# A selective-scan layer on one core: two elementwise additions moved to DMAs, eight states instead of six added up by DMAs, and the order of the step written anew

## What is computed

```python
mod = (_silu(L0_c) @ L0_wmod).reshape(B, 6, 1, -1)          # sa, ca, ga, sb, cb, gb
h = _layernorm(x) * (1 + ca) + sa
xz = h @ w_in.T + b_in;  x_ssm, z = split(xz);  z = silu(z)
dt = softplus(x_ssm @ w_dt.T + b_dt)
Bm, Cm = x_ssm @ w_B.T + b_B, x_ssm @ w_C.T + b_C
# for each position: h_n = exp(A_n * dt) * h_n + dt * Bm_n * x_ssm ;  y = sum_n h_n * Cm_n   (n = 0..15)
y = (y + D * x_ssm) * z
pre = y @ w_out.T + b_out + h
x = x + ga * (normalised(pre) * gamma + beta)
h = _layernorm(x) * (1 + cb) + sb
x = x + gb * feed_forward(h)        # 512 -> 64, 64 small functions of one variable, 64 -> 512
```

## Time and profile before

| | |
|---|---|
| median of 3 runs | 4297.14 us (4292.26 to 4300.26) |
| the profiled execution | 4280.81 us, of which the span of the profile 4279.1 us |
| busy, share of the span | PE 96%, ACT 89%, DVE 85%, POOL 83% |
| granted TensorE clock | 0.989 of full speed, 1.00 in all of the middle |
| length of a step | 128.7 us |
| traffic | 555.86 MB by DMA, of which 302.02 MB on POOL's queue |

### The profile page before, as it was taken

One profiled execution on the slowest core, in us unless ns is written; L12 is line 12 of the kernel. 1 busy time (PEld: TensorE's weight loads), 2 busy tenths in 40 slices (PEclk: granted clock), 3 DMA queues, 4 the chain that ended last, 5 costly groups with the idle time before them and its releaser, 6 DMA issues. The chain is left out here.

```text
span 4279.1 us, 70886 instructions
## 1 busy us (share of the span) xinstructions
PE 4100.2 (96%) x22688; PEld 2620.3 (61%) x22688; DVE 3643.8 (85%) x5134; ACT 3826.7 (89%) x6371; POOL 3558.1 (83%) x2090
## 2 busy tenths in 40 slices
PE   7999999999999999999999999999999999999987
PEld 3666666666666666666666666656666666666654
DVE  3788898888888888888888888888988888988884
ACT  3899999999999999998999999999999999999984
POOL 2888889888888888888888888988888888888883
PEclk8999999999999999999999999999999999999998
DMA  4456555656655666555666555665556675556663
GB/s 148 103 125 150 133 122 110 145 131 145 135 123 111 142 141 141 133 115 117 139 148 141 128 115 126 134 148 132 128 115 137 133 150 132 125 113 141 129 140 70
DMA packets 242537, 555.86 MB, mean 130 GB/s; under 512 B 29020, under 2 KB 31068, under 8 KB 242168
## 3 DMA queue, kind: packets, MB, share of 16 engines
q0 software_dynamic: 98816, 302.02, 39.1%
q1 hardware_dynamic: 143352, 249.29, 18.9%
HBM read 281.70 MB, written 34.64 MB: 74 GB/s over the span
## 5 line engine op out<-in xcount | busy, mean ns | idle before, releaser
L411 POOL TENSOR_TENSOR work<-work,c_bc 128x1024 f32<-128x1024 f32 x1024 | 2653.2, 2672 | 414.2 <-DVE work L1219 307.0
L1219 DVE TENSOR_TENSOR_SCAN work<-work,state,b_ps 128x512 f32<-128x512 f32 x1792 | 2245.6, 1272 | 242.2 <-PE b_ps L526 207.1
L925 ACT ACTIVATE work<-u_td,b_td 128x512 f32<-128x512 f32 x2048 | 1455.5, 711 | 114.7 <-PE b_ps L526 104.7
L915 ACT ACTIVATE work<-dt_t,neg_a 128x512 f32<-128x512 f32 x2048 | 1453.9, 710 | 17.1 <-DVE work L1219 14.7
L526 PEld LDWEIGHTS b_ps<-ident,work 128*128 128x128 f32 x8192 | 969.1, 141 | 645.1 <-issue 415.5
L526 PE MATMUL b_ps<-ident,work 128*128 128x128 f32 x8192 | 1229.1, 275 | 107.6 <-DVE work L1219 100.3
L601 PEld LDWEIGHTS y_ps<-ident,work 128*128 128x128 f32 x5120 | 585.9, 141 | 164.1 <-issue 157.1
L601 PE MATMUL y_ps<-ident,work 128*128 128x128 f32 x5120 | 673.4, 275 | 4.6 <-DMA work<-work 2.8
L675 PE MATMUL dense<-w_out_t,proj 128*128 128x512 f32 x1024 | 519.7, 606 | 0.0
L733 PE MATMUL dense<-xs_t,w_dt_t 128*128 128x512 f32 x1024 | 506.1, 593 | 0.0
L767 PE MATMUL dense<-h_t,w_in_t 128*128 128x512 f32 x1024 | 502.7, 593 | 0.0
(11 more groups left out here) (113 smaller groups left out, 4214.4 us busy)
## 6 DMA issues: line engine op xcount, KB each, us to landing
work<-work POOLq DMA_DIRECT2D x384, 512.0 KB, 5.7
c_bc<-c_d SPq DMA_DIRECT2D x512, 256.0 KB, 3.5
xn<-in_x SPq DMA_DIRECT2D x128, 256.0 KB, 5.1
work<-xs_t POOLq DMA_DIRECT2D x64, 512.0 KB, 5.9
x<-in_x SPq DMA_DIRECT2D x128, 256.0 KB, 4.4
x<-par_d POOLq DMA_DIRECT2D x64, 512.0 KB, 6.7
x<-par_d POOLq DMA_DIRECT2D x32, 1024.0 KB, 9.9
out_dram<-x SPq DMA_DIRECT2D x128, 256.0 KB, 4.2
```

Source lines behind the costliest of these rows:

```text
L411: gp.tensor_tensor(made_here, both(hs, HS_RING, s * U + i), c_bc[:, (s * N + n) % C_RING:(s * N + n) % C_RING + 1, :].to_broadcast([P, 2, ...
L915: A(decay[:, (s * U + i) % DEC_RING, :], dt_t[:, s % 2, j, :], ACT.Exp, scale=neg_a[:, j, n:n + 1]).then_inc(S["dec_done"], 1)
L925: A(v[:, n % V_RING, tb, :], u_td[:, tb, :], ACT.Copy, scale=b_td[:, s % 2, tb, n:n + 1]).then_inc(S["v_done"], 1)
L1219: V.tensor_tensor_scan(hs[:, (s * U + i) % HS_RING, :], decay[:, (s * U + i) % DEC_RING, :], b_ps[:, i % 2, :], state[:, i:i + 1] if s % N ...
```

## The change

1. `HELD` goes from 6 to 8 states. `add_products` issues 16 DMAs a step instead of 12 (each adds 512 KB to 512 KB), and `add_unit` on PE runs 32 times instead of 40.
2. `attended`: ACT writes `t2` straight into `x1`, and a DMA per two tiles adds x plus shift to it. x plus shift is made ahead in a DRAM buffer `xsh_d`: SP copies the shift row over it (`spread_shift`), POOL's queue adds the whole chunk of x (`add_x`). SP's four loads and POOL's two `shifted` DMAs fall away, and so do POOL's four additions.
3. `step_size`: two DMAs of 512 KB instead of four additions on POOL.
4. `turn_x2` is one group later, inside `dt.0` to `dt.3` instead of `xs.3` to `dt.2`.
5. All of `PE_AT` and `AT` is written anew.

```diff
-    HELD = (0, 1, 3, 4, 6, 8)
+    HELD = (0, 1, 3, 4, 6, 7, 9, 10)
...
-    for entry in """g.0@0 g.1@0 g.2@0 g.3@0 g.4@1 g.5@2 g.6@2 yz.0@2 g.7@3 res.0@3 yz.1@3 pre.0.0@4 yz.2@4 pre.0.1@5
+    for entry in """g.0@0 g.1@0 g.2@2 g.3@2 g.4@8 g.5@8 g.6@8 yz.0@8 g.7@9 res.0@9 yz.1@10 pre.0.0@10 yz.2@10 pre.0.1@11
...
+        xsh_d = nc.dram_tensor("xsh_d", (2, TB, P, D), f32).ap()
...
-            def loads(b, c):
-                for tb in range(TB):
-                    yield AT["load"][tb]
-                    sp.wait_ge(S[f"stored_{tb}"], at(f"stored_{tb}", c, Q))
-                    sp.dma_start(x1[:, tb, :], ap["x"][b * T + tb * P:b * T + (tb + 1) * P, :]
-                                 ).then_inc(xb_loaded[tb], Q)
+            def spread_shift(s):
+                yield AT["spread"]
+                sp.wait_ge(S["par_stored"], 4 * Q)
+                if s >= 2:
+                    for n in range(TB // 2):
+                        sp.wait_ge(x1_added[n], (s - 1) * Q)
+                sp.dma_start(xsh_d[s % 2].rearrange("b p d -> p b d"),
+                             par_d[1:2, s // NC:s // NC + 1, :].to_broadcast([P, TB, D])
+                             ).then_inc(S["shift_spread"], Q)
...
-            def shifted(b):
+            def add_x(s):
+                yield AT["x_add"]
+                gp.wait_ge(S["shift_spread"], (s + 1) * Q)
+                gp.dma_start(xsh_d[s % 2].rearrange("b p d -> p b d"),
+                             ap["x"][s * T:(s + 1) * T, :].rearrange("(b p) d -> p b d", p=P),
+                             accum_op=ALU.add).then_inc(S["x_added"], Q)
+
+            def attended(b):
                 for n in range(TB // 2):
-                    yield AT["xsh"][n]
-                    gp.wait_ge(S["par_stored"], 4 * Q)
-                    for tb in (2 * n, 2 * n + 1):
-                        gp.wait_ge(xb_loaded[tb], (b + 1) * Q)
-                    gp.dma_start(x1[:, 2 * n:2 * n + 2, :], par_d[1:2, b // NC:b // NC + 1, :].to_broadcast([P, 2, D]),
-                                 accum_op=ALU.add).then_inc(xsh_done[n], Q)
-
-            def attended(b):
-                for tb in range(TB):
-                    yield AT["x1"][tb]
-                    gp.wait_ge(xsh_done[tb // 2], (b + 1) * Q)
-                    gp.wait_ge(S["t2_done"], at("t2_done", b, tb + 1))
-                    gp.tensor_tensor(x1[:, tb, :], x1[:, tb, :], tmp[:, tb, :], ALU.add
-                                     ).then_inc(S["x1_done"], 1)
+                    yield AT["x1"][n]
+                    gp.wait_ge(S["x_added"], (b + 1) * Q)
+                    gp.wait_ge(S["t2_done"], at("t2_done", b, 2 * n + 2))
+                    gp.dma_start(x1[:, 2 * n:2 * n + 2, :], xsh_d[b % 2, 2 * n:2 * n + 2].rearrange("b p d -> p b d"),
+                                 accum_op=ALU.add).then_inc(x1_added[n], Q)
...
-                for m in range(KD):
-                    yield AT["dt_add"][m]
-                    gp.wait_ge(S["ldt_done"], at("ldt_done", f, m + 1))
-                    gp.tensor_tensor(dt_t[:, f % 2, m, :], dt_t[:, f % 2, m, :], tmp[:, m, :], ALU.add
-                                     ).then_inc(S["dt_done"], 1)
+                for n in range(KD // 2):
+                    yield AT["dt_add"][n]
+                    gp.wait_ge(S["ldt_done"], at("ldt_done", f, 2 * n + 2))
+                    gp.dma_start(dt_t[:, f % 2, 2 * n:2 * n + 2, :], tmp[:, 2 * n:2 * n + 2, :], accum_op=ALU.add
+                                 ).then_inc(dt_added[n], Q)
...
-                to = inside(s, ("xs.3", "dt.0", "dt.1", "dt.2")[j])
+                to = inside(s, ("dt.0", "dt.1", "dt.2", "dt.3")[j])
...
+                    act.wait_ge(S[f"stored_{tb}"], at(f"stored_{tb}", b - 1, Q))
+                    A(x1[:, tb, :], tmp[:, tb, :], ACT.Copy, scale=norm[:, 1, tb, 8:9]
                       ).then_inc(S["t2_done"], 1)
```

More of the change, by code:

```diff
@@ L86, in build_program @@
-        st2=(23, 23, 23, 24),
-        nmr2=25,
-        y=(14, 14, 18, 24, 28, 28, 34, 34, 36, 37, 40, 40, 45, 46, 46, 46, 46, 46, 46, 47, 47, 51, 52, 52, 54, 54, 55, 56, 57, 61, 61, 61, 62, 62, 62, 62, 62, 64, 64, 64),
-        sum=(6, 8, 9, 11, 13, 17, 17, 20, 21, 25, 30, 32, 39, 40),
+        store=(5, 10, 13, 18),
+        c_store=54,
+        x1=(18, 26),
+        bout=57,
+        dt_add=(49, 52),
+        u_mul=(54, 54, 56, 56),
+        gate=(38, 62, 63, 10),
+        relu=(63, 63, 2, 2, 2, 2, 7, 8),
@@ new lines, in build_program @@
+        gm=9,
+        skip=(12, 12, 12, 15),
+        rstdx=20,
+        xn=(20, 20, 20, 20),
+        t2=(18, 20, 24, 25),
+        rstd2=37,
+        xn2=(37, 37, 37, 37),
+        h2=(40, 45, 47, 50),
+        h=(22, 25, 26, 28),
+        xs=(32, 34, 37, 38),
+        cb=54,
+        bt=54,
+        edt=(46, 48, 50, 51),
+        ldt=(46, 48, 50, 51),
+        ez=(29, 59, 60, 10),
+        lz=(32, 59, 60, 10),
+        sig=(35, 59, 60, 10),
+        y_copy=(7, 7, 7, 7),
+        yz=(9, 10, 11, 13),
@@ new lines, in build_program @@
+        out=(14, 16, 17, 20),
+        pre=(15, 18, 20, 24),
+        dt=(43, 46, 49, 51),
+        ut=(60, 61, 62, 62),
+        z=(27, 59, 61, 63),
+        s=62,
+        stx=(9, 15, 16, 18),
+        nmrx=19,
+        st2=(29, 32, 36, 37),
+        nmr2=37,
+        y=(15, 18, 18, 18, 31, 31, 32, 34, 40, 42, 42, 42, 50, 50, 51, 52, 54, 55, 55, 56, 56, 57, 58, 58, 62, 63, 63, 63, 63, 64, 68, 68),
+        sum=(5, 8, 9, 11, 13, 16, 17, 20, 23, 25, 30, 31, 36, 37, 42, 44, 45, 48),
+        spread=19,
@@ L90, in build_program @@
+        x_add=63,
     )
@@ L359, in step @@
                     chains.append(stores(c))
-                if has_b:
-                    chains.append(loads(b, c))
+                if has_s:
+                    chains.append(spread_shift(s))
                 if has_f:
@@ L504, in step @@
                 if has_b:
-                    chains += [last_gate(b), shifted(b), attended(b), add_bout(b)]
+                    chains += [last_gate(b), attended(b), add_bout(b)]
                 if has_b and b % NC == 0:
@@ L839, in dense @@
                             turn_x(s, f, b, 3)
-                        if has_b and (m, k) == (3, 1):
-                            yield slot("x2", 0)
-                            turn_x2(s, f, b, 0)
                 for m in range(KD):
@@ L847, in dense @@
                             add_dt(s, f, b, m, k)
-                        if has_b and m < 3 and k == 1:
-                            yield slot("x2", m + 1)
-                            turn_x2(s, f, b, m + 1)
+                        if has_b and k == 1:
+                            yield slot("x2", m)
+                            turn_x2(s, f, b, m)
                 if has_f:
@@ L853, in dense @@
                         yield slot("cb", k)
-                        add_cb(s, f, k)
+                        add_cb(s, f, b, k)
                 for k in range(KD):
```

102 lines of the change are left out of this document (33 added, 69 removed).

## The result

The changed kernel takes 4274.01 us (median of 4 runs, 4273.07 to 4274.83), the kernel before 4295.69 us beside it (4 runs, 4292.26 to 4300.26): a ratio of 0.9949, 95% interval 0.9932 to 0.9966. It is faster, as forecast, and inside the range, but by 22 us and not by the 88 of the sum.

A forecast was written before the change was run, and what follows sets the result against it. PE was taken to set the pace for most of a step, DVE and ACT at its start. -112 + 19 + 5 = -88 us from the profiled 4280.8 gave 4193, plus 16 for the median: 4209 us (-2.0%), range 4130 to 4300.

The forecast's parts named there:

- the 88 of the sum: Whole kernel: -112 for eight held states, +19 for the new order, +5 for the fill, giving -88 us.
- The DMA case: DMA engines become the bound; PE's y units of state 11 wait for late sums, +131 us, 4340 us; chance 0.14.
- What the trace would show: Changed profile: L603 4,096 instructions, about 540 us; step near 125.5 us; POOL near 80% or below; DMA share near 0.75 mid-step.
- One sign of being wrong: Waits of PE's y units or of POOL for `work<-work` of 100 us or more, with L426 landings well above 5.7 us.
- the ACT rival: ACT becomes the bound, its waits for PE's `bt` and for copies growing by 1.5 and 1.2 us a step; 4283 us; chance 0.12.
- The eight units: Eight y units of four transposes leave PE each step where it is full: 3.5 us a step, -112 us.
- This gives back from 0 to 1.2 us a step. I take half, 0.6: Rewritten tables: more PE idle at a step's start, a long PE piece at its end; costs +19 us over 31 steps.
- the 5.1 us forecast: Slots 0 to 7: PE stands still for 5.1 us instead of 3.9, with 7.0 us of work against DVE's 12.1.
- the rival: DMA engines become the bound: sums of state 11, issued at slots 45 and 48, reach PE's additions late; 4340 us, chance 0.14.
- gets no more than it has: Slots 8 to 26, DMA share already 0.92 and 0.99: no added load, as new DMAs go to stretches of 0.60 and 0.14.
- a mean share of 0.79: DMA engines' share of a step, up from 0.60 by 4 MB more on POOL's queue; would still fit, wherever the bytes lie.
- Fill: Start of the program: `u` waits for a DMA landing after 5.7 or 6.7 us instead of a 1.26 us addition, +5 us.

The follow-up runs named there:

- a_undo_held: The changed kernel with six held states again (four DMAs of 512 KB a step fewer, eight y units more on PE): 4397.01 us, 1.0247 of before.
- a_spread56: The changed kernel with SP's 1 MB spread of the shift row issued at slot 56 instead of 19: 4242.02 us, ratio 0.9885 to before.
- a_short_stats: The changed kernel with DVE's statistics of x over 8 of 512 channels (first norm wrong): 4266.45 us, ratio 0.9936 to before.

## Why the prediction was right and wrong

- **Direction**: right. The DMA case, slower at 4340 us, did not come; the y units waited 19.9 us for the sums in all and not 131 (their weight loads, which overlap PE, 50.9).
- **What the trace would show**: PE's count and POOL's share came as told. L603 is at 558.7 us (some 540 told), the DMA share is 0.76 (0.75 told), but the step is 128.2 us (125.5 told). One sign of being wrong came: POOL waited 118.2 us for `work<-work`, over the 100 named, though the median landing was 5.5 us. ACT's waits for `b_td` and `u_td` stayed under the 6 us a step named (4.6), but those for `u_td` grew by 2.6 us a step, where the ACT rival had 1.2.
- **The eight units** (-112 us, "These units lie where PE is full, so their time counts"): in the new order the size held (122 us, a_undo_held, with the limit named there). As a reason it did not: in the order of before eight units lie where PE is full and gave 46 us.
- **The step that failed** is the cost of the new order: "This gives back from 0 to 1.2 us a step. I take half, 0.6". By the pitches, PE has 122.8 us of work in the 129.2 of a step before and 119.3 in the 128.2 of the changed kernel, so its loss grew from 6.4 to 8.9 us, by 2.5 and not 0.6: -3.5 + 2.5 = -1.0 us, as measured. 0.9 of the 2.5 is the jam that a_spread56 removes, and 1.6 is the order itself, though the DMAs for `dt` alone brought about 0.9. Measured by a_undo_held, part 1 gives 4.3 us a step and parts 2 to 5 cost 3.3.
- **Where the order's part lies** is worked out as an estimate: the length of each stretch less the matmuls that start in it, each at its pitch (mean of the steps 4 to 28, in us). The difference is PE's loss:

```
slots            0      8     16     24     32     40     48     56    step
before         3.4    1.1    0.3    0.6   -0.2    0.8    0.4    0.0     6.4
changed        3.5    2.4    1.4    0.4    0.3    0.7    0.2    0.1     8.9
a_spread56     3.5    2.4    1.4    0.4    0.0    0.1    0.1    0.1     8.0
```

  Slots 0 to 7 lose what they lost before, and not the 5.1 us forecast: PE runs ahead of the scans, so most of the `g` of slot 8 falls into them. Slots 8 to 23, which I did not look at, lose 2.4 us more. `g`, `yz` and `res` moved there, but so did DVE's copies and statistics, and DVE is busy for 15.97 of 16.16 and 16.52 of 17.42 us. a_short_stats shows that DVE binds in slots 8 to 15, and that lifting it gives 0.9 us in place and 0.3 a step. For slots 16 to 23 no run tests it.
- **The transfers**: the rival asked whether a y unit would find its sum late. The stretch of slots 8 to 26, I wrote, "gets no more than it has", as `shifted` and SP's loads leave it. The spread of 1 MB, which has "44 slots", stands right in it. It was never late itself; it made others late: sums landed after up to 15.8 us, and POOL, which works in order, stood ahead of the next sum for 118 us. I had costed POOL and the spread at nothing. That a mean share of 0.79 would still fit was my own conclusion, and where the bytes lay mattered. The Trainium skill (DMA: Bandwidth & Descriptors, "Rules for kernel authors") says only that DMAs issued from several engines run on the same 16 engines. The trace agrees: a copy on SP's queue made the sums on POOL's queue late (up to 15.8 us, and 7.7 with the copy 37 slots later).
- **Fill** (+5): 10.9 us to the first copy of `ut` and 17.1 with the first two steps. The DMAs for `dt`, on which the +5 rests, have 2.1 of it; 4.2 to 8.1 are the fourth statistic behind the products at slot 16, a place that no table shows since it is written in the generator. The 6.2 us of the first two steps stay open.

The sum again with what was measured, in medians: -122 for part 1, +32 for the jam, +7 for the products in the fill, and a remainder of +61 for the order and the rest of the fill, give the measured -22. The remainder is worked out as the difference and has the limit of a_undo_held's split. Its steps alone would make it larger, as the order costs 3.3 - 0.9 = 2.4 us a step there, 74 us in 31 steps; against that, part 1 is 4.3 x 31 = 133 us in the steps, of which 10 are lost in the fill and from the last step on.

## What to carry to other kernels

A share of "24.00 of 24" says that an engine has no time to spare, not that taking work from it gives time: where it exchanges a two-deep ring with another engine, freed time can turn into waiting for the ring, as the rows above are read. Price such an edit by leaving the work out in place, both in the old order and the new, before believing the pitch times the count; here eight units were worth 46, 28, 25, 23 and 122 us, by their place and by what stood around them.

When an order is rewritten, make the tally of each engine for each eight slots of the new order and take the greatest; the engine that was the bound in the old one is not enough. And place a transfer with slack by what lands beside it, not by when it is needed: the harm is to its neighbours, their longest landings show it where the DMA share doesn't, and one number, from slot 19 to 56, was worth more than the change.

## What the runs showed of the hardware that was not expected

- A 1 MB copy from DRAM to DRAM on SP's queue took 13.2 us to land in the full stretch and 11.1 us at slot 56; the 1 MB addition in DRAM took 8.6 and 10.3.
- A copy on SP's queue lengthens landings on POOL's: with its 1 MB issued at slot 19 instead of 56, the longest landing of a 512 KB sum was 15.8 us instead of 7.7, at nearly the same median (5.5 and 5.2).
- The granted clock was 1.00 in all eight stretches of a step of the kernel before, though PE stood still for 2.4 of 17.03 us in its slots 0 to 7. In the changed kernel it was 0.93 and 0.95 in slots 0 to 15, thus for a part of them at the lower of its two levels (1.2 and 2.4 GHz), with PE idle for 2.0 of 12.1 us. What it cost wasn't separated.
